# The mask of a cross-attention's transposed scores: two identity products on TensorE, or one add on VectorE

## What is computed

```python
scores = jnp.einsum('bsgrd,btgd->bgrst', xq, xk) / math.sqrt(HEAD_DIM)
scores = scores + mask
probs = jax.nn.softmax(scores.astype(jnp.float32), axis=-1).astype(q.dtype)
out = jnp.einsum('bgrst,btgd->bsgrd', probs, xv)
```

## Time and profile before

| | |
|---|---|
| three runs | 431.54, 433.43, 433.76 us, median 433.43 us |
| the profiled execution | 430.7 us, span 428.9 us |
| PE busy | 342.3 us in 2661 instructions |
| DVE busy | 272.3 us in 974 |
| ACT busy | 154.0 us in 293 |
| POOL busy | 110.4 us in 203 |
| mean granted clock of PE | 0.88 of full speed |

### The profile page before, as it was taken

How to read it: one execution, slowest core, us unless ns; L and a number is a source line. 1 busy time by engine, 2 the same in 40 slices (tenths; PEclk the granted TensorE clock), 3 DMA queues, 4 the chain that set the end, 5 groups by cost and what they waited for, 6 DMA issues and landing times.

```text
span 428.9 us, 7568 instructions
## 1 busy us (share of the span) xinstructions
PE 342.3 (80%) x2661; PEld 241.6 (56%) x2661; DVE 272.3 (63%) x974; ACT 154.0 (36%) x293; POOL 110.4 (26%) x203
## 2 busy tenths in 40 slices
PE   2074768998796899997999999979889978399463
PEld 2074645677563565885756758956455656244242
DVE  1616475245754974766789748687885787843635
ACT  3513122632022475431136663313357522036220
POOL 3026041023131212343223304524212432100221
PEclk9999755699696999995999999989999995669758
DMA  8904930006867001068641101596300034300001
GB/s 287 355 11 161 249 86 23 5 11 202 222 145 177 7 4 30 6 204 229 153 127 44 54 11 51 182 270 156 105 17 4 2 108 120 100 2 3 0 1 50
DMA packets 22255, 42.58 MB, mean 99 GB/s; under 512 B 7449, under 2 KB 11777, under 8 KB 20681
## 3 DMA queue, kind: packets, MB, share of 16 engines
q1 hardware_dynamic: 21945, 41.58, 34.8%
q10 hardware_dynamic: 272, 0.52, 0.3%
HBM read 29.32 MB, written 12.32 MB: 97 GB/s over the span
## 4 chain that ended last, share of the span: by engine, by line
PE 51%; DVE 21%; DMA 11%; issue 5%; SPq 5%; ACT 3%; POOL 3%; DVEq 0%; POOLq 0%; ACTq 0%
DVE x L763 9%; PE bank_a L868 6%; PE bank_a L869 6%; PE bank_a L870 6%; DMA ks<-scr_k 5%; DVE nma L699 4%; PE bank_a L948 3%; PE bank_b L1013 3%; PE bank_b L1002 3%; PE bank_a L935 3%; PE bank_b L1005 2%; PE bank_b L1003 2%; PE bank_b L1048 2%; DMA c_in<-in_ctx_dram 2%; PE bank_b L1049 2%
## 5 line engine op out<-in xcount | busy, mean ns | idle before, releaser
L763 DVE CUSTOM_DVE_ANT_0 x<-bank_b,mraw 128x128 f32<-128x128 f32 x256 | 59.2, 287 | 11.2 <-PE bank_b L990 4.9
L584 ACT ACTIVATE pb<-bank_b 128x512 f32<-128x512 f32 x64 | 38.0, 597 | 68.5 <-PE bank_b L1005 49.3
L699 DVE TENSOR_REDUCE nma<-bank_a 128x4 f32<-128x512 f32 x64 | 39.6, 681 | 8.6 <-PE bank_a L918 8.5
L576 ACT ACTIVATE pa<-bank_a 128x512 f32<-128x512 f32 x64 | 37.2, 597 | 21.6 <-PE bank_a L948 10.8
L990 PE MATMUL bank_b<-kx,qx 96*128 96x128 bf16 x256 | 27.1, 256 | 14.3 <-DVE nmb L763 7.4
L868 PE MATMUL bank_a<-xH,wH 128*128 128x256 f32 x128 | 37.1, 290 | 0.0
L869 PE MATMUL bank_a<-xL,wH 128*128 128x256 f32 x128 | 36.7, 286 | 0.0
L870 PE MATMUL bank_a<-xH,wL 128*128 128x256 f32 x128 | 36.6, 286 | 0.0
L1002 PE MATMUL bank_b<-idr,mH 128*128 128x512 f32 x64 | 35.9, 561 | 0.5 <-DVE nmb L763 0.5
L918 PE MATMUL bank_a<-ks,qs 96*128 96x128 bf16 x256 | 25.3, 250 | 8.7 <-DMA ks<-scr_k 7.2
L990 PEld LDWEIGHTS bank_b<-kx,qx 96*128 96x128 bf16 x256 | 18.8, 113 | 22.7 <-DVE nmb L763 11.1
(11 more groups left out here) (160 smaller groups left out, 727.5 us busy)
## 6 DMA issues: line engine op xcount, KB each, us to landing
wraw<-in_L_attn_attn_qkvw_dram SPq DMA_DIRECT2D x3, 1024.0 KB, 8.5
scr_q<-qp SPq DMA_DIRECT2D x4, 768.0 KB, 3.6
scr_k<-kp SPq DMA_DIRECT2D x4, 768.0 KB, 4.2
qs<-scr_q SPq DMA_DIRECT2D x4, 768.0 KB, 7.1
ks<-scr_k SPq DMA_DIRECT2D x4, 768.0 KB, 10.5
scr_x<-xp SPq DMA_DIRECT2D x8, 384.0 KB, 2.7
qx<-scr_x SPq DMA_DIRECT2D x8, 384.0 KB, 4.0
qs<-scr_q SPq DMA_DIRECT2D x4, 512.0 KB, 9.0
```

The source lines that it names most:

```text
L576: act.activation(pa[:, n % NP, :], pa_bank(i, *step)[:], ACT.Exp, scale=HD ** -0.5).then_inc(*ra.is_empty(i, *step))
L584: act.activation(pb[:, n % NPB, :], pb_bank(i, *step)[:], ACT.Exp).then_inc(*rb.is_empty(i, *step))
L699: dve.tensor_reduce(nma[:, b, 4 * j:4 * j + 4], pa_bank(i, *step)[:].rearrange("p (m t) -> p m t", m=KT), AX.X, ALU.max, negate=True).then ...
L763: last = dve.tensor_tensor_reduce(x2[:, b, r * P:(r + 1) * P], pb_bank(i, *step)[:, r * P:(r + 1) * P], mraw[:], -1.0, -LOWEST, ALU.add, A ...
```

## The change

DVE adds the mask, transposed once into the SBUF tile mT, to the finished scores in their PSUM bank, as one tensor_tensor over 128x512 elements in place; the mask tile is read four times through a broadcast pattern. The two products with the identity go, and the score product alone opens and closes the bank. ACT waits for the new semaphore mask_added in place of the bank's full. Step C0.mask takes a bank now (it leaves NO_BANK): PE transposes mraw there and DVE copies it to mT; mH, mL and idr go with their three DVE operations. ORDER is as it was.

```diff
-NO_BANK = ("xb", "lc", "cp", "ldq", "ldk", "ldx", "ldc", "n1", "n2", "n3", "w", "ow", "mask", "sign", "rows", "scales")
+NO_BANK = ("xb", "lc", "cp", "ldq", "ldk", "ldx", "ldc", "n1", "n2", "n3", "w", "ow", "sign", "rows", "scales")
...
-        mH = sb("mH", [P, P], F32R)
-        mL = sb("mL", [P, P], F32R)
+        mT = sb("mT", [P, P], F32)
...
-        idr = sb("idr", [P, P], F32R)
...
# ACT, step st of B
-                        rb.wait_full(act, i, *step)
+                        act.wait_ge(mask_added, n + 1)
...
# DVE
+                elif thread == "B" and name == "st":
+                    b, g = step[1:]
+                    rb.wait_full(dve, i, *step)
+                    if i == 0 and b == 0 and g == 0:
+                        rb.wait_emptied(dve, 0, "mask")
+                    d4 = pb_bank(i, *step)[:].rearrange("p (r t) -> p r t", r=4)
+                    dve.tensor_tensor(d4, d4, mT[:].rearrange("p (o t) -> p o t", o=1).broadcast_to([P, 4, P]), ALU.add).then_inc(mask_added, 1)
...
                 elif thread == "C" and name == "mask":
-                    dve.wait_ge(ld_mask, 16)
-                    dve.tensor_copy(mH[:], mraw[:]).then_inc(masks, 1)
-                    dve.wait_ge(masks, 1)
-                    dve.tensor_tensor(mL[:], mraw[:], mH[:].bitcast(F32), ALU.subtract).then_inc(masks, 1)
-                    dve.wait_ge(idents, 1)
-                    dve.tensor_copy(idr[:], idf[:]).then_inc(masks, 1)
+                    rb.wait_full(dve, 0, "mask")
+                    dve.tensor_copy(mT[:], pb_bank(i, "mask")[:, 0:P]).then_inc(*rb.is_empty(i, "mask"))
...
# PE, step st of B
                         if i == 0:
                             pe.wait_ge(rows_b, 16 * GB)
-                            pe.wait_ge(masks, 3)
...
-                    ident4 = idr[:].rearrange("p (o t) -> p o t", o=1).broadcast_to([P, 4, P])
-                    pe.matmul(d4, mH[:], ident4, start=True, stop=False)
-                    pe.matmul(d4, mL[:], ident4, start=False, stop=False)
                     a = 4 * (g % 2)
-                    pe.matmul(d4, kx[0:SM, b, g, :], qx[0:SM, b, a:a + 4, g // 2, :], start=False, stop=True).then_inc(*rb.is_full(i, *step))
+                    pe.matmul(d4, kx[0:SM, b, g, :], qx[0:SM, b, a:a + 4, g // 2, :], start=True, stop=True).then_inc(*rb.is_full(i, *step))
...
+                elif thread == "C" and name == "mask":
+                    rb.wait_free(pe, 0, "mask")
+                    pe.wait_ge(ld_mask, 16)
+                    pe.wait_ge(idents, 1)
+                    pe.transpose(pb_bank(i, "mask")[:, 0:P], mraw[:], idf[:]).then_inc(*rb.is_full(i, "mask"))
```

More of the change, by code:

```diff
@@ L275, in decoder_layer @@
         idents, w_high, w_low = sem("idents"), sem("w_high"), sem("w_low")
-        ow_high, ow_low, signs, masks = sem("ow_high"), sem("ow_low"), sem("signs"), sem("masks")
+        ow_high, ow_low, signs, mask_added = sem("ow_high"), sem("ow_low"), sem("signs"), sem("mask_added")
         scale_step, scales, ones_a, ones_b, picks = sem("scale_step"), sem("scales"), sem("ones_a"), sem("ones_b"), sem("picks")
```

## The result

The changed kernel takes **472.9 us** (median of 4 runs, 471.4 to 478.0), the kernel before 433.3 us beside it. The ratio is 1.099, with a 95% interval of 1.093 to 1.104: 39.6 us slower, where 20.1 were forecast, and 9.9 above the upper end of the range (463). The profiled execution of after is the longest of its four (478.0 us, span 476.2), so lags that are read from its trace run some 5 us above the median.

A forecast was written before the change was run, and what follows sets the result against it. The bound was taken to alternate between VectorE and TensorE by stretch. Queue delays of 18.3 us plus 1.8 us of half clock made 20.1 us on the 433.4 us median: 453.5 us, range 441 to 463.

The forecast's parts named there:

- The bound and the sign: Whole kernel: bound changes between VectorE and TensorE stretch by stretch; change makes it slower, chance 0.88.
- sentence on the drain: VectorE adds: by it, each of some 45 on the path would cost 0.09 us more, 4 us in all.
- What the removal gives: TensorE's 128 mask products: 62 us busy time, at most 22 us on the path; none credited in the sum.
- The queue term: Cross-attention score steps: adds in VectorE's in-order queue delay exps, copies and pv steps, +18.3 us over all groups.
- Group 0: First sixteen score steps: some adds hide in VectorE's waits; its two runs of eight cost +1.2 and +2.2 us.
- Group 1: Second sixteen score steps: adds ahead of maxima and routing; its two runs of eight cost +4.8 and +2.0 us.
- Group 2: Third sixteen score steps: adds in VectorE's queue less some idle time, +7.3 us, no clock cost.
- 2,0: First eight score steps of Group 2: seven adds before a self-attention score step, one after, less idle time: +3.8 us.
- 2,1: Last eight score steps of Group 2: eight adds before the routing's last operation, delaying TensorE's transpose: +3.5 us.
- Group 3: Last sixteen score steps: adds replace the products on the path, +0.8 us queue and +1.8 us clock.
- The step that failed is the clock term: Last run's pv steps: half clock lasts over two of them, 1.94 us instead of 1.06 each, +1.8 us.
- The rival of the falling clock: More stretches: adds thin out TensorE's work; two more spells at half clock, 3.5 us each, giving 460.5 us; chance 0.2.

The follow-up runs named there:

- the fill: Kernel with adds in group 2 alone, plus 31 filler products ahead of two score steps and one later step where TensorE idled: 440.9 us, against 445.7 unfilled.
- the filled one: Changed kernel with filler products ahead of the third product at six places, and ahead of a later step in groups 0 and 2: 465.8 us.

## Why the prediction was wrong in size

**The bound and the sign held.** VectorE's full stretches carried the adds onto the path, the exps wait for them (76.1 us), no mask product is left in the chain and the adds have the 5% of it that was forecast. An add lasts 690 ns and four in a row 2.50 us, that is 0.69 + 3 x 0.60, as priced by L815 and L699. The Trainium skill's sentence on the drain (VectorE: DVE Perf Modes, The DRAIN you can't avoid), that an operation starts only when the pipe is empty, is not what the adds into PSUM show: they overlap by 0.09 us. But the same paragraph of the Trainium skill goes on that an operation which is not held starts earlier, and with that the 0.09 us agree; the prediction took half of the paragraph when it called the trace at odds with it.

**What the removal gives** was counted at nothing, and nothing is what came of it: without the add the kernel is at 1.000 of before. The reason was in part luck, since the few microseconds that the trace does gain go again at half clock.

**The queue term, 18.3 us, was near, and a little low.** It can be read from the four traces with adds in one group, as the growth of TensorE's lag less what is put down to the clock below. Group 0: 3.9 us (3.4 forecast); across the two adds among the maxima VectorE's lag goes from -0.6 to +0.6, the 1.2 forecast. Group 1: 7.4 (6.8). Group 2: 3.8 us in 2,0 (3.8) and 4.0 in 2,1 (3.5). Group 3: 1.5 us (0.8), the last four adds behind ot:0,1's layer norm as described, but that norm ending later. Together 20.6 us.

**The step that failed is the clock term:** "the half clock to last over two of the last run's pv steps, 1.94 us instead of 1.06 each: +1.8". The mechanism was named, at one place of eight. The forecast took it that TensorE had enough work in the other runs because the granted clock there was 1.00 before; but that row had the very products that the change removes. With the add in, the mean clock is 0.861 with two products left at each step and 0.786 without. What the runs show in its place, group by group:

- Group 3: three pv steps took 1.94 us, 2.6 us for the 1.8.
- Group 2, forecast at 0: two pv steps of 2,0 took 1.94 us, 1.8 us in all, and in 2,1 the fill takes back 4.5.
- Group 1, forecast at 0: pv steps of 1.94, 1.93 and 1.61 us, 2.3 us in all. Its median came within 0.6 us of the forecast, but its trace has 9.7 us, near 6.8 and these 2.3; that the median agreed is in part luck.
- Group 0, forecast at 0: the three pv steps that took 1.06 us before take 1.93 or 1.94, 2.6 us; and twice TensorE runs on at half clock with no add in between, from B0.pv:0,1 to A1.st:1,5 (lag 1.7 to 3.6) and from B0.pv:1,1 to A1.pv:1,7 (8.4 to 11.2), 4.7 us.

These are 18.5 us where 1.8 were forecast. They are a reading of lags that lie 1 to 3 us a group above the medians, so they are nearer the top than the middle. And the first spell of group 0 need not be the add's: in the filled kernel of group 2, whose program up to there is that of before, TensorE waited 1.47 us for a transfer at 145.63, ran from 147 to 154 us at 0.51, and its lag grew by 2.9 us with no add there.

The rival of the falling clock had the mechanism, and the mean granted clock of 0.786 against 0.878 shows it. The section of the Trainium skill on bank cycling (TensorE: Matmul & The Clock Gate, A second HAM failure mode: psum-queue depth-cycling) describes such a fall, and the trace agrees with that number. The rival's price of two spells of 3.5 us, 7.0 in all, was too small by more than half.

**TensorE's busy time** was forecast at 280 us and is 355.0: it was worked out at the old clock.

**What stays open.** By the mean clocks, TensorE stands at half clock for 105 us of before's span, 204 of after's and 129 of the run with two products at each step. That run thus took back three quarters of the added half clock and only 5.6 us (7.7 by the ratios) of the time. Either its products, which stand behind a freed bank, cost most of what the clock gave, or much of the added half clock falls where it costs nothing and the queue's part in the whole kernel is above 20.6 us; no run tells the two apart. The four groups alone sum to 32.6 us and the whole is 39.6; each difference is uncertain by some 2 to 3 us, so up to half of the 7 may be nothing. That half clock at the end of one group reaches into the next is a guess that no run tested. Nor is the clock's total measured by a run: the fill gave back 4.8 us of group 2's 14.0 and 7.0 of the whole 39.6, and left other spells at half clock both times. Between the chips of those two runs of group 2 the kernel before differed by 1.6 us; by the ratios, 1.030 and 1.019, the fill gave back the same 4.8, but their intervals overlap, and it is the windows and the pv steps above that carry the claim.

No version with the add beat the kernel before. The best of them that adds the whole mask is the filled one, at 465.8 us.

## What to carry to other kernels

Work that looks covered may be what keeps TensorE's clock up: before taking products away, look at what TensorE does in the same microseconds afterwards, and add to the cost of each new idle stretch (here 2.0 to 4.7 us) what the next busy stretch loses at half clock (here up to 4.4 us). An engine put between product and consumer costs by its place in the queue: read when that engine would come to the new instruction, not only how long it lasts. And where a step of work moves to an engine, run it in one part of the kernel at a time; four such runs located most of the error, which the whole could not.

## What the runs showed that I had not expected

The fill of group 2 adds 31 fp32r products of 512 columns to TensorE, and the kernel gets faster (445.7 to 440.9 us; in all groups, with 62 products more, 472.9 to 465.8). Leaving out all mask work, 62 us of TensorE's busy time, moved the time by no more than its interval. And a VectorE add over 256 columns lasts 426 ns where 512 last 690: (690 - 426) / 256 is 1.03 ns a column and 162 ns fixed, by a line through two lengths. Whether its sum goes to PSUM or to SBUF makes 8 ns of difference (690 and 682).
